# First attention of a small vision tower: rotary scales and offsets folded into tables by GpSimd

## The reference, cut to what matters

```python
x = (query - mu) * rsqrt(var + 1e-05) * ln_w + ln_b
u = silu(x @ Wu + bu)
v = silu(x @ Wv + bv)
base = silu(x @ Wbase + bbase)             # 128 features
q = _rope(base * q_w + q_b)                # q_w, q_b: one number per feature
k = _rope(base * k_w + k_b)
qk = einsum('bms,bns->bmn', q, k)
kernel = square(relu(qk / mpe + bias))
out = u * einsum('bmn,bne->bme', kernel, v) @ Wo + bo

def _rope(x):                              # x1, x2: the two halves of the features
    return concatenate([x1 * cos - x2 * sin, x2 * cos + x1 * sin])
```

## Time and profile before

| | |
|---|---|
| Time, median of 3 runs | 159.64 us (159.57 to 159.81) |
| The profiled execution's own time | 160.54 us |
| Its span, first to last instruction | 158.7 us |
| Mean granted clock of TensorE | 0.988 |
| TensorE matmuls busy | 141.8 us, 89% |
| VectorE busy | 99.5 us, 63% |
| ScalarE busy | 73.5 us, 46% |
| GpSimd busy | 33.0 us, 21% |

### The profile page before, as it was taken

One profiled execution on the slowest core, in us unless ns is written; L12 is line 12 of the kernel. 1 busy time (PEld: TensorE's weight loads), 2 busy tenths in 40 slices (PEclk: granted clock), 3 DMA queues, 4 the chain that ended last, 5 costly groups with the idle time before them and its releaser, 6 DMA issues.

```text
span 158.7 us, 2893 instructions
## 1 busy us (share of the span) xinstructions
PE 141.8 (89%) x1099; PEld 72.1 (45%) x1112; DVE 99.5 (63%) x306; ACT 73.5 (46%) x138; POOL 33.0 (21%) x84
## 2 busy tenths in 40 slices
PE   6999789999999999789995996999899999999970
PEld 1546355645454344345552312466344555554450
DVE  7424777764548728576464899962848467413982
ACT  3656951775545010177237000525683167377542
POOL 8700000047778000005300003400069000000000
PEclk9999999999999999999999997899999999999999
DMA  5999980000000000000001000000000000000001
GB/s 168 344 423 347 261 333 14 4 0 2 2 4 2 0 0 0 0 4 0 0 19 41 0 2 0 0 4 0 0 0 4 0 2 0 4 0 0 4 0 37
DMA packets 3700, 8.04 MB, mean 51 GB/s; under 512 B 1579, under 2 KB 1707, under 8 KB 3558
## 3 DMA queue, kind: packets, MB, share of 16 engines
q1 hardware_dynamic: 3478, 7.78, 14.7%
q10 hardware_dynamic: 208, 0.07, 0.2%
HBM read 7.48 MB, written 0.15 MB: 48 GB/s over the span
## 4 chain that ended last, share of the span: by engine, by line
PE 63%; DVE 21%; ACT 8%; issue 4%; DMA 2%; SPq 0%; DVEq 0%; ACTq 0%
PE ps L403 14%; PE ps L463 10%; PE ps L450 7%; DVE scores L1311 6%; PE ps L457 4%; PE ps L410 3%; DVE residual L1430 3%; PE ps L418 2%; DMA k_parts_img<-k_parts_tok 2%; DVE patch_sb L1422 2%; PE ps L571 2%; PE ps L563 1%; ACT hidden L887 1%; PE ps L432 1%; PE ps L614 1%
## 5 line engine op out<-in xcount | busy, mean ns | idle before, releaser
L403 PE MATMUL ps<-idle_operand 128*128 128x512 bf16 x124 | 36.5, 408 | 5.3 <-DVE scores L1311 1.7
L1137 DVE TENSOR_TENSOR hidden_gated<-hidden,ps 128x576 f32<-128x576 f32 x28 | 19.7, 750 | 10.3 <-PE ps L457 10.3
L887 ACT ACTIVATE hidden<-ps,weights_sb 128x576 f32<-128x576 f32 x28 | 19.6, 738 | 11.0 <-PE ps L450 8.3
L403 PEld LDWEIGHTS ps<-idle_operand 128*128 128x128 bf16 x137 | 12.3, 105 | 19.6 <-issue 6.4
L879 ACT ACT_TABLE_LOAD x16 | 20.5, 1283 | 0.3
L867 ACT ACTIVATE squares<-ps 128x288 f32<-128x288 f32 x8 | 3.3, 411 | 31.3 <-PE ps L655 8.4
L463 PE MATMUL ps<-hidden_gated,weights_sb 128*64 128x288 f32 x112 | 16.3, 418 | 0.0
L318 POOL CAST combine_parts_T<-combine_parts_T 48x288 f32<-48x288 bf16 x3 | 1.3, 420 | 62.5 <-DVE combine_parts_T L1105 62.5
L450 PE MATMUL ps<-h,weights_sb 64*128 64x288 f32 x80 | 13.1, 436 | 0.6 <-ACT hidden L887 0.4
L1073 DVE COPY centred<-ps 128x288 f32<-128x288 f32 x8 | 3.7, 457 | 13.0 <-ACT squares L867 13.0
L463 PEld LDWEIGHTS ps<-hidden_gated,weights_sb 128*64 128x64 f32 x112 | 6.7, 136 | 7.0 <-DVE hidden_gated L1137 2.4
(11 more groups left out here) (286 smaller groups left out, 226.7 us busy)
## 6 DMA issues: line engine op xcount, KB each, us to landing
patch_sb<-patches SPq DMA_DIRECT2D x6, 288.0 KB, 5.1
weights_sb<-weights SPq DMA_DIRECT2D x1, 1108.0 KB, 10.0
weights_sb<-weights SPq DMA_DIRECT2D x1, 717.0 KB, 15.1
weights_sb<-weights SPq DMA_DIRECT2D x1, 689.0 KB, 13.9
weights_sb<-weights SPq DMA_DIRECT2D x1, 640.0 KB, 7.2
weights_sb<-weights SPq DMA_DIRECT2D x1, 512.0 KB, 13.0
weights_sb<-weights SPq DMA_DIRECT2D x1, 394.0 KB, 14.2
weights_sb<-weights SPq DMA_DIRECT2D x1, 375.5 KB, 6.4
```

The lines of the kernel that those rows point to most:

```text
L403: mm(PS[:, bank, :], idle_in[:, 0:P], idle_in[:, :], start=True, stop=True)
L887: act.activation(HR[:, at % RING, :, :], two(ZA if ch % 2 == 0 else ZB), func, bias=w(f"b1_{n}")[:, ch:ch + 1]).then_inc(S["act_out"], 1)
L1137: dve.tensor_tensor(HG[:, at % GRING, :, :], HR[:, at % RING, :, :], two(GATE_AT[n][ch]), ALU.mult)\
```

## The change

GpSimd makes eight small tables of 128x36 as soon as the constants and the weights a0 have landed: cosine and sine tables times the scales (four, `rope_tables`), and the same times the offsets (four, `rope_bias`), the latter then added pairwise to two. DVE multiplies B1 and B2 directly with the scaled tables. GpSimd adds the offset tables to QP and KP over all 576 tokens, in place, and DVE adds QP and QS, KP and KS as before. ACT's four affine copies are gone. In TensorE's stream the residual now stands ahead of the wait for q_ready, with five filling matmuls before it and three behind that wait, instead of eight and four.

```diff
+        RT, RB = sb("rope_tables", [P, 4, POS]), sb("rope_bias", [P, 4, POS])
...
+        def imgs(x):
+            return x[:, :].rearrange("p (b n) -> p b n", b=IMAGES)
+
+        def each_image(table):
+            return table.unsqueeze(1).to_broadcast([P, IMAGES, POS])
...
+            pool.wait_ge(S["const"], 16)
+            pool.wait_ge(S["w_a0"], 16)
+            for n, (table, name) in enumerate((("rope_c", "q_w"), ("rope_c", "k_w"), ("rope_s", "q_w_sw"), ("rope_s", "k_w_sw"))):
+                pool.tensor_scalar(RT[:, n, :], c(table), w(name), None, ALU.mult).then_inc(S["rope_tab"], 1)
+            for n, (table, name) in enumerate((("rope_c", "q_b"), ("rope_c", "k_b"), ("rope_s", "q_b_sw"), ("rope_s", "k_b_sw"))):
+                pool.tensor_scalar(RB[:, n, :], c(table), w(name), None, ALU.mult).then_inc(S["rope_tab"], 1)
+            pool.wait_ge(S["rope_tab"], 8)
+            for n in range(2):
+                link(pool.tensor_tensor(RB[:, n, :], RB[:, n, :], RB[:, n + 2, :], ALU.add))
+            for n, x in enumerate((QP, KP)):
+                pool.wait_ge(S["rope_cos"], n + 1)
+                pool.tensor_tensor(imgs(x), imgs(x), each_image(RB[:, n, :]), ALU.add).then_inc(S["rope_add"], 1)
 
             gates32(0)
...
             pe.wait_ge(S["silu_base"], 2)
-            idle(8, G)
-            pe.wait_ge(S["q_ready"], 1)
-            idle(4, G)
+            idle(5, G)
             pe.wait_ge(S["silu_u"], 1)
             pe.wait_ge(S["hp"], 1)
             residual("ident")
+            pe.wait_ge(S["q_ready"], 1)
+            idle(3, G)
             pe.wait_ge(S["k_ready"], 1)
...
             act.wait_ge(S["silu_base"], 2)
-            for dst, src, nm_ in ((QP, B1, "q_%s"), (QS, B2, "q_%s_sw"), (KP, B1, "k_%s"), (KS, B2, "k_%s_sw")):
-                act.activation(dst[:, :], src[:, :], ACT.Identity, bias=w(nm_ % "b"), scale=w(nm_ % "w"))\
-                   .then_inc(S["rope_in"], 1)
             act.wait_ge(S["proj_v"], 1)
...
-            dve.wait_ge(S["rope_in"], 1)
-            step(dve.tensor_tensor(imgs(QP), imgs(QP), tab_c, ALU.mult))
-            dve.wait_ge(S["rope_in"], 2)
-            link(dve.tensor_tensor(imgs(QS), imgs(QS), tab_s, ALU.mult))
+            dve.wait_ge(S["rope_tab"], 8)
+            dve.wait_ge(S["silu_base"], 1)
+            dve.tensor_tensor(imgs(QP), imgs(B1), each_image(RT[:, 0, :]), ALU.mult).then_inc(S["rope_cos"], 1)
+            dve.tensor_tensor(imgs(KP), imgs(B1), each_image(RT[:, 1, :]), ALU.mult).then_inc(S["rope_cos"], 1)
+            dve.wait_ge(S["silu_base"], 2)
+            link(dve.tensor_tensor(imgs(QS), imgs(B2), each_image(RT[:, 2, :]), ALU.mult))
+            dve.wait_ge(S["rope_add"], 1)
             dve.tensor_tensor(QF[:, :], QP[:, :], QS[:, :], ALU.add).then_inc(S["q_ready"], 1)
-            dve.wait_ge(S["rope_in"], 3)
-            step(dve.tensor_tensor(imgs(KP), imgs(KP), tab_c, ALU.mult))
-            dve.wait_ge(S["rope_in"], 4)
-            link(dve.tensor_tensor(imgs(KS), imgs(KS), tab_s, ALU.mult))
+            link(dve.tensor_tensor(imgs(KS), imgs(B2), each_image(RT[:, 3, :]), ALU.mult))
+            dve.wait_ge(S["rope_add"], 2)
             dve.tensor_tensor(KF[:, :], KP[:, :], KS[:, :], ALU.add).then_inc(S["k_ready"], 1)
```

More of the change, by code:

```diff
@@ L84 @@
 lru_exp lru_ang lru_sin lru_tab
-proj_base proj_base_sw proj_v proj_u silu_base silu_v silu_u rope_in q_ready k_ready qk_done kern_ready ctx_done uc_ready
+proj_base proj_base_sw proj_v proj_u silu_base silu_v silu_u rope_tab rope_cos rope_add q_ready k_ready qk_done kern_ready ctx_done uc_ready
 logits exp_in exp_out onehot counted comb_split comb_turned comb_t ctf_ready gates z_done act_out gated y_done
```

## The result

The kernel became slower, and its times spread. Six executions took 161.99 to 173.23 us, median 165.31; the kernel before took 159.09 to 159.81, median 159.6. A second set of six gave 161.17 to 165.55, median 162.36 against 160.08, ratio 1.0133 (1.0084 to 1.0182). Forecast were 159.8 us and a range of 158.0 to 161.3; both medians lie above that range, so the prediction was wrong.

What follows compares the result with a forecast made beforehand. Bound: ACT's chain to the residual (21.35) and DVE's to K ready (21.21), both ahead of Q·K. ACT's 3.15 us and DVE's 1.5 earlier are eaten by 1.9 of GpSimd: 159.64 + 0.1 = 159.8 us, range 158.0 to 161.3.

Steps and rivals of the forecast that it cites:

- ACT's copies and the residual: First attention: four affine copies go, 3.15 us; residual done at 18.3, leaving the path by 3 us.
- Tables: GpSimd's eight 128x36 instructions ready at 13.9, 1.3 us before DVE's first product at 15.24; costed at nothing.
- DVE without GpSimd: Six 128x576 instructions before Q·K start at 15.24 instead of 16.77; K ready at 19.61, 1.60 us earlier.
- Collision: DVE's two-SBUF-operand instructions and GpSimd's two adds exclude each other: 2·0.94 less 0.26 us, K ready at 21.35.
- Clock: TensorE idles some 2.3 of 3.1 us before Q·K; the sum counts no clock fall, given a chance of 0.30.
- Rival 1: TensorE's clock falls around 20.5 to 21.8 us, over real work behind Q·K: 1.5 us, 161.3 us; chance 0.30.
- rival 3: Late tables, or adds of 1.3 to 1.73 us blocking whole: K ready 22.2 to 23.1, 160.6 to 161.5 us; chance 0.08.

Runs made afterwards that it cites:

- e1_no_adds: Changed kernel without GpSimd's two large adds and DVE's waits for them, offsets of Q and K left out: 159.21 us, ratio 0.9938 to before.
- e6_write_only: Changed kernel with GpSimd's two large adds replaced by fills with zeros that read nothing, offsets left out: 158.70 us, ratio 0.9935 to before.
- e7_psum: Changed kernel with Silu results left in PSUM, so DVE's six instructions have one SBUF operand; fillers moved: 159.18 us, ratio 0.9948 to before.
- e3_dve_adds: Changed kernel with the two offset adds on DVE instead of GpSimd, fillers five, two and eight: 160.11 us, ratio 1.0015 to before.
- e4_before_no_fill: Kernel before with five fillers instead of eight ahead of the q_ready wait, none instead of four behind: 161.52 us, ratio 1.0068 to before.
- after_again: Changed kernel run once more, unaltered: 162.36 us, ratio 1.0133 to before.
- e2_fill: Changed kernel with eleven more fillers between residual and q_ready wait, six instead of three behind it: 161.04 us, ratio 1.0064 to before.
- e8: Changed kernel with GpSimd's add for Q alone, offset of K left out, fillers five, six and five: 159.91 us, ratio 1.0006 to before.

## Why the prediction was wrong, point by point

Two terms of the sum failed. GpSimd's adds were taken to hold DVE up by 1.62 us (1.74 with what is lost at each handing over), and held it up by 2.27. And TensorE's clock was put at nothing in the sum, though the forecast itself had TensorE idle for 2.3 us; it cost 4.5 us in the one profile and 1.5 in the other. The second is the larger one.

- **ACT's copies and the residual: right.** The residual started at 18.30, 3.2 us after Silu of base, where 3.1 was forecast. That path left the chain.
- **Tables: right.** They were ready 1.5 us before DVE wanted them, where 1.3 was forecast.
- **DVE without GpSimd: right.** Forecast 1.60 us earlier; e1_no_adds and e6_write_only gave 1.56.
- **Collision: mechanism right, size wrong.** The step "I take for an add the part that grows with length, 576·1.6 = 0.94 us, and let its start hide in the gaps" failed. Measured are 1.40 us for an add, 1.20 and 1.07 of it as standing time of DVE. The slope between 288 and 320 elements was drawn over 32 elements and carried over 256. The trace of before had a nearer row, which the prediction didn't use: tensor_tensor instructions of 512 elements on GpSimd (on one partition) take 1.15 us, which in proportion is 1.30 for 576. This is one of them in the groups by shape (busy us, mean ns):

```profile
L392 POOL TENSOR_TENSOR bias_rest<-bias_rows,bias_bf 1x512 f32<-1x512 f32 x1 | 1.2, 1157 | 0.1
```

With whole adds of 1.30 less the 0.26 of the gaps K would have been ready at 21.95, and measured, put on the start of before, is 21.96. It came 0.75 us late instead of 0.14.

- **Clock: right as a rival, wrong as a term of nothing and as a chance.** TensorE was forecast to idle 2.3 us and idled 2.75, more than at either wait of the earlier trace rows, and one of those two was followed by a fall. A chance of 0.30 was low for that, and the range ended at the rival's own middle, 161.3. The rival read the fall of before as coming during the wait; the clock is 1.00 to the wait's end at 96.74 and falls at 96.9. Its price, 1.5 us for a fall of 3.4 us, was right (6.23 - 4.71 = 1.52), though it was partly luck: a third of 1.92 is 0.64, not the 0.4 that went into it. That a fall can last 10.2 us wasn't considered.
- **The sum of both was left out.** Rival 1 took the forecast's collision of 0.1 us and rival 3 a large one with the clock up. Both came. With the short fall they make 0.76 + 1.52 = 2.3 us, which gives 161.9 where the second set's median is 162.4; with the long one 0.76 + 4.5 = 5.3 us, which gives 164.9 where the profiled execution took 165.28. Either lies above the range's 161.3.

## What to carry to other kernels

In this kernel, work moved from ACT to GpSimd didn't run beside DVE's work as long as both read SBUF and DVE had two operands there: their times added up, and the profile showed it as longer instructions, not as waits. Three ways out were measured: one operand in PSUM (e7_psum), the adds on DVE itself (e3_dve_adds), and, where the work allows it, GpSimd only writing (e6_write_only). When a change makes TensorE wait longer, fill the waits again and measure once more before judging the change: here the clock cost more than the collision.

## What the runs showed of the hardware that wasn't expected

- The clock's fall is a matter of the single execution: the same e4_before_no_fill took 159.79 and 170.01. Once down it stayed for 3.4 us in one profile (22.7 to 26.1) and for 10.2 in another (23.0 to 33.3), though TensorE was busy in nearly all of both. Why the second lasted longer stays open.
- The slowest executions must have had more low clock than any profile shows. An estimate: since the low level is half the high one, a mean of 0.920 over a span of 169.9 us means 27 us at the low level. The same working gives 10.8 us for the profiled execution of the changed kernel, in which 10.2 are seen in the first attention. Where the 27 us lie isn't shown.
- A GpSimd add of 576 elements takes 1.40 us with plain and with broadcast operands, a tensor_tensor of 320 elements 0.72: 2.6 ns for each further element, where 288 to 320 gave 1.6.
- The scatter of up to 1 us between like executions sits in two places in the profiles: the start of Silu of base, and a wait for the K transfers before the scores. From the copy at the fifth layer norm (L1073 before) to the first score reduction (L1311 before) it is 10.0 us in before and e1_no_adds, 10.1 in after_again, and 9.1 in after, e2_fill, e6_write_only and e7_psum; the longer ones are those in which TensorE waits for these transfers. That is why e1_no_adds, with 137.3 us from Q·K to the end, gains nothing there against before's 137.4, and e2_fill, e6_write_only and e7_psum have 136.4 to 136.5.
- A third part lies outside the span. It is 1.7 to 1.9 us in all executions of before that ran beside the experiments, but up to 2.8 in e1_no_adds, 2.9 in e7_psum and 3.3 in the changed kernel. By the medians of the spans e1_no_adds gained 1.15 us and e7_psum 1.0, more than the 0.7 and 0.6 by the medians of the times. What it is isn't shown. Such scatter hides gains of half a microsecond, which is why e3 and e8 can't be told from before by time, though their stretch is 0.22 and 0.35 us shorter.
